# Four tiles of a graph layer summed from gathered rows by GpSimd and VectorE, not by products on TensorE

## The reference

```python
# graph part, x is (6250, 256), a self loop is added to every node
deg = segment_sum(ones, dst);  dis = rsqrt(deg);  norm = dis[src] * dis[dst]
for l in range(2):
    x_res = x
    h = x @ W[l]
    agg = segment_sum(norm[:, None] * h[src], dst) + b[l]
    x = relu(agg + x_res @ resW + resb)
# expert part, on layernorm(x): 6 experts of three 256x256 products, top 2
rh = relu(features @ router_w1 + router_b1)
top_w, top_i = top_k(softmax(rh @ router_w2 + router_b2), 2)
combined = sum(expert_out[top_i] * softmax(top_w))
```

## Time and profile before

| | |
|---|---|
| median of 3 runs | 2027.67 us (2026.81 to 2027.71) |
| profiled execution | 2028.8 us, its span 2027.2 us |
| TensorE busy | 1845.7 us of the span |
| VectorE busy | 1120.7 us |
| ScalarE busy | 771.5 us |
| GpSimd busy | 387.4 us |
| moved by DMAs | 412.55 MB, 124.85 MB of it from GpSimd's queue |

### The profile page before, as it was taken

One profiled execution on the slowest core, in us unless ns is written; L12 is line 12 of the kernel. 1 busy time (PEld: TensorE's weight loads), 2 busy tenths in 40 slices (PEclk: granted clock), 3 DMA queues, 4 the chain that ended last, 5 costly groups with the idle time before them and its releaser, 6 DMA issues. The chain is left out here.

```text
span 2027.2 us, 34554 instructions
## 1 busy us (share of the span) xinstructions
PE 1845.7 (91%) x11170; PEld 1128.0 (56%) x11170; DVE 1120.7 (55%) x2788; ACT 771.5 (38%) x1686; POOL 387.4 (19%) x403
## 2 busy tenths in 40 slices
PE   4448799999999999999959999999999988998886
PEld 3336555555555555555524445444454476886775
DVE  7246766666666666666504444444444566644443
ACT  2226755665566655665501222222222232221221
POOL 1680000000000000000000211111211133335664
PEclk8769899999999999999979999999999999998998
DMA  6255399998999972323364555444555556767783
GB/s 221 58 85 111 106 330 308 285 333 257 293 293 272 282 248 94 153 108 134 154 274 159 184 193 203 173 174 170 184 202 196 186 183 200 253 214 234 256 254 123
DMA packets 121920, 412.55 MB, mean 204 GB/s; under 512 B 14633, under 2 KB 75009, under 8 KB 115577
## 3 DMA queue, kind: packets, MB, share of 16 engines
q1 hardware_dynamic: 82936, 283.65, 40.2%
q0 software_dynamic: 37904, 124.85, 21.9%
q10 hardware_dynamic: 1008, 3.21, 0.4%
HBM read 201.60 MB, written 219.99 MB: 208 GB/s over the span
## 5 line engine op out<-in xcount | busy, mean ns | idle before, releaser
L1383 PE MATMUL bank<-parts,counts 128*128 128x512 f16 x2401 | 643.3, 378 | 0.0
L1383 PE MATMUL bank<-parts,counts_again 128*128 128x512 f16 x2401 | 540.3, 381 | 18.5 <-DMA counts_again<-counts_table 18.5
L1547 ACT ACTIVATE counts<-bank 128x392 f16<-128x392 f32 x800 | 395.1, 497 | 311.2 <-PE bank L1463 304.5
L1383 PEld LDWEIGHTS bank<-parts,counts_again 128*128 128x128 f16 x2401 | 234.1, 99 | 288.4 <-issue 17.0
L594 DVE TENSOR_TENSOR rows_lo<-pair_keys,iota_lo 128x2048 bf16<-128x2048 bf16 x200 | 244.9, 1225 | 239.4 <-PE bank L1463 239.3
L1463 PEld LDWEIGHTS bank<-rows_hi,rows_lo 128*128 128x128 bf16 x3200 | 227.6, 99 | 203.7 <-issue 27.1
L1463 PE MATMUL bank<-rows_hi,rows_lo 128*128 128x98 bf16 x3200 | 277.8, 210 | 11.3 <-DVE rows_hi L594 10.5
L1383 PEld LDWEIGHTS bank<-parts,counts 128*128 128x128 f16 x2401 | 192.5, 96 | 103.6 <-issue 1.1
L454 POOL DMA_INDIRECT first_rows<-route_rows,route_spot_i x49 | 47.9, 977 | 825.7 <-DVE tokens L445 817.7
L594 DVE TENSOR_TENSOR rows_hi<-pair_keys,iota_hi 128x1568 bf16<-128x1568 bf16 x200 | 193.5, 967 | 0.0
L2261 DVE TENSOR_SCALAR h_t<-bank,counts_again 128x256 f32<-128x256 f32 x120 | 57.7, 483 | 161.4 <-PE bank L2097 115.6
(11 more groups left out here) (259 smaller groups left out, 1843.1 us busy)
## 6 DMA issues: line engine op xcount, KB each, us to landing
counts_table<-counts SPq DMA_DIRECT2D x25, 3136.0 KB, 13.7
counts_again<-counts_table SPq DMA_DIRECT2D x24, 3136.0 KB, 11.4
counts_again<-expert_pack SPq DMA_DIRECT2D x60, 898.0 KB
first_rows<-zero_rows POOLq DMA_DIRECT2D x3, 10530.0 KB, 58.4
second_rows<-zero_rows POOLq DMA_DIRECT2D x3, 10449.0 KB, 70.2
res_tile<-res_table SPq DMA_DIRECT2D x98, 128.0 KB, 6.5
first_rows<-zero_rows POOLq DMA_DIRECT2D x1, 10270.0 KB, 61.8
second_rows<-zero_rows POOLq DMA_DIRECT2D x1, 10191.0 KB, 66.7
```

The source lines that it names most:

```text
L1383: mm = nc.tensor.matmul(acc[:, 0:2 * dim], lhs, rhs, start=s == 0, stop=s == tiles)
L1547: nc.scalar.activation(counts[:, b, :, :].rearrange("p s (o n) -> p o s n", o=2)[:, :, :, q * QUAD:(q + 1) * QUAD], bank[4 + q % 4][:, 0:Q ...
```

## The change

Pairs 18 and 20 (`GATHERED`, the tiles 36, 37, 40 and 41) get no one-hot rows, no counts and no products with counts, in either layer. Instead:

- A table `message_table[l]` in DRAM holds the messages in 32 bits (6,272 rows of 256, and 128 rows of zeros). For layer 0 it is written in the preparation: GpSimd adds `rest` and the high half of each tile (49 additions of 128x256), and SyncE stores the result in 7 chunks. For layer 1 the node update stores its scaled row too (one more DMA of 128 KB per tile).
- For each of the four tiles, 56 slots of source nodes (`source_of`) are made from a gathered run of the edge list; unused slots point to a row of zeros. GpSimd's queue then fetches the rows: per layer 28 groups of 8 indirect DMAs (128 rows of 1 KB each), 224 in all, and 4 direct ones for the self loops, into a ring of 3 buffers (`fetch_group`). VectorE sums each group and the running sum in one reduction over the slots of a 128 x 9 x 256 buffer (`sum_group`, 28 per layer).
- In layer 0 VectorE sums two groups per pair in the pairs 2 to 15. In layer 1 GpSimd issues four groups first and then one or two after each pair's scatters.
- The update and the routing of the gathered tiles stay, and are placed among the products of the pairs 19, 21 and 22 by a list written out by hand; the row buffers of the router become three, with a second PSUM bank.
- The packing of the weights moves from GpSimd in the preparation to SyncE at the start of layer 0. The large stores of zeros are gone: the experts' tables have one block of zero rows in front of each region (12 small DMAs), and an expert's last block starts earlier, so that it reads no row that was not written.

The core of the diff:

```diff
+    GATHERED = (18, 20)
+    BACK = 2 * len(GATHERED)
+    RUN = 56
+    LATE = GATHERED[0]
...
+        SLOTS, RING = 8, 3
...
+        def fetch_group(pool, ring, l, n):
+            g = l * GROUPS_ALL + n
+            m, T = tile_of(g)
+            if g >= RING:
+                pool.wait_ge(ring_summed, g - RING + 1)
+            pool.sem_inc(pool_link, 1)
+            if g % GROUPS_OF == 0:
+                pool.dma_start(ring[:, g % RING, 0, :], message_table[l][T * P:(T + 1) * P, :]).then_inc(ring_filled[g % RING], 16)
+            for k in range(SLOTS):
+                at = g % GROUPS_OF * SLOTS + k
+                pool.indirect_dma_start(ring[:, g % RING, k + 1, :], None, message_table[l],
+                                        bass.IndirectOffsetOnAxis(ap=source_of[:, m, at:at + 1], axis=0)).then_inc(ring_filled[g % RING], 16)
+
+        def sum_group(dve, ring, l, n):
+            g = l * GROUPS_ALL + n
+            m, T = tile_of(g)
+            dve.wait_ge(ring_filled[g % RING], fills(g))
+            if g > 0:
+                dve.wait_ge(ring_summed, g)
+            to = gathered_sums[:, m, :] if g % GROUPS_OF == GROUPS_OF - 1 else ring[:, (g + 1) % RING, 0, :]
+            nc.vector.tensor_reduce(to, ring[:, g % RING, :, :].rearrange("p s d -> p d s"), AX, ALU.add).then_inc(ring_summed, 1)
...
+                def message_row(t):
+                    pool.wait_ge(rest_ready, t + 1)
+                    nc.gpsimd.tensor_tensor(feat[:, t, :], rest[:, t % 4, :], parts[:, t, 0:dim], ALU.add).then_inc(message_made, 1)
+                    pool.wait_ge(message_made, t + 1)
...
                 def rest_of(t):
                     dve.wait_ge(high_ready, t + 1)
-                    if t >= 2:
-                        dve.wait_ge(middle_ready, t - 1)
...
+                    if t >= 4:
+                        dve.wait_ge(middle_ready, t - 3)
+                        dve.wait_ge(message_made, t - 3)
...
     def store_next(self, eng, T, o):
         eng.wait_ge(self.res_out, T + 1)
+        eng.wait_ge(self.messages_ready, T + 1)
...
+        eng.dma_start(self.message_table[self.l + 1][bass.ds(T * P, P), :], self.scaled[:, o, :]).then_inc(self.res_stored[o], 16)
...
+            GROUPS_BESIDE = range(2, 2 + GROUPS_ALL // 2)
...
+                            if n in GROUPS_BESIDE and r in (2, 6):
+                                sum_group(dve, ring, 0, 2 * GROUPS_BESIDE.index(n) + (r == 6))
...
                     update.load(sp, 0, 0, 0)
+                    pack_weights(sp)
                     store_counts(0, 0)
...
                 @block.gpsimd
                 def _(pool):
-                    store_zeros(pool)
+                    for n in range(GROUPS_ALL):
+                        fetch_group(pool, ring, 0, n)
                     update.wait_stored(pool)
...
+        LATE_ROUTES = {19: ((17, ROUTE_AT), (18, (92, None, None, None))),
+                       21: ((18, (None, 6, 14, 34)), (19, (44, 52, 60, 92))),
+                       22: ((20, (4, 12, 20, 40)), (21, (50, 58, 66, 94))),
+                       23: ((22, ROUTE_AT),),
+                       24: ((23, ROUTE_AT[0:3] + (None,)),)}
...
+        FIRST_GROUPS = 4
+
+        def groups_behind(p):
+            first = FIRST_GROUPS + (3 * p + 1) // 2
+            return range(min(first, GROUPS_ALL), min(FIRST_GROUPS + (3 * p + 4) // 2, GROUPS_ALL))
+
+        def groups_beside(i):
+            if i in (1, 2):
+                return range(2 * i - 2, 2 * i)
+            return groups_behind(i - 3)
...
+                    for n in range(FIRST_GROUPS):
+                        fetch_group(pool, work.ring, 1, n)
+                    for p in range(LAST_PAIR - 1):
+                        router.scatter(pool, p, buffer_of(p), 2)
+                        for n in groups_behind(p):
+                            fetch_group(pool, work.ring, 1, n)
```

More of the change, by code:

```diff
@@ L1582, in pair @@
[L1582 to L1587 removed]
+                                    update.turned_copy(act, first, 0)
+                                if q == (30 if gathered_tiles else 28):
+                                    update.high_part(act, first, 0, pair_at(n - 1))
+                    for n in range(4):
+                        pair(n, n // 2, n % 2)
```

779 lines of the change are left out of this document (511 added, 268 removed).

## The result

The changed kernel takes 2212.8 us (median of 4 runs, 2200.22 to 2225.03) against 2027.69: 1.0896 times as long, with a 95% interval of [1.0854, 1.0938]. The forecast was 1958 with a range of 1925 to 2130; the time lies above it.

What follows compares the result with a forecast made beforehand. TensorE's list was taken to bound both layers. From 2028.8 us, savings of 55.1 and 43.2, plus 4 for layer 1's start and 24 for late releases, gave 1958.5, predicted as 1958; range 1925 to 2130.

Steps and rivals of the forecast that it cites:

- Late releases, 24 us: Layer 0: ScalarE's copies released late beside 28 groups of eight gathers, 0.86 us each, 24 us in all.
- point (c): Layer 1's scatters, four indirect DMAs in a row, showed no late releases in the trace before the change.
- The same step in layer 1: 0 us: Layer 1: late releases charged nothing, as a released sum has 11 us; 24 more allowed in the range.
- layer 1 hides all 28: Layer 1: VectorE, busy in only 265 of 596 us, absorbs its 28 new reductions at no cost.
- The reduction's length, 2.6 us: VectorE: one reduction of 2,304 elements takes 2.6 us by the longer row, 4.1 by the Trainium skill's hopping rule.
- the 9 to 17 feared: Layer 0: loss if reductions take longer, 9 us at 3.8 us each or 17 at 4.1; 0 was taken.
- TensorE's savings, 98.3 us: Products dropped for two gathered pairs save 55.1 us in layer 0 and 43.2 in layer 1.
- SyncE, 0 us: Start of layer 0: 52 DMAs ahead of the first store of counts, 0.47 us each, cost 0, up to +10.
- The preparation, 0 us: Preparation: GpSimd's 49 new additions and the moved weights cost 0 in all, range -8 to +8.
- The start of layer 1, 4 us: Start of layer 1: 14 gathers, 1.8 MB, arrive beside the data TensorE waits for; +4 us, 0 to +8.
- rival 2: GpSimd bounds layer 1, its indirect DMAs slowed to 1.6 us beside VectorE's two-input operations; 1995 us; 13%.
- rival 1: Late releases bound both layers and make the kernel slower, between 2033 and 2400 us, most below 2150; 26%.

Runs made afterwards that it cites:

- e16: e15 with four kinds of fetch per layer, one per tile (plain, direct, 16-byte rows, 64 rows, pauses); 2095.36 us, 1.0318 times the kernel before.
- e1: The changed kernel without any fetches, the ring filled once with zeros, reductions and waits kept; 1960.35 us against 1963.43 for the kernel before, ratio 0.9981.
- e12: e8 with layer 1's first reduction of a pair moved ahead of shift_logits; 1926.82 us against 1958.88 for the kernel before, ratio 0.9832.
- e7: The changed kernel with the reduction over nine neighbouring elements in place of slots 1 KB apart; 2170.81 us, 39 us less than e6.
- e15: The changed kernel with weights packed by GpSimd after layer 0's last gather and layer 1's first reduction moved; 1899.54 us against 1961.79 for the kernel before.
- e5: The kernel before, unchanged, traced on the same machine as e6; 2022.1 us, with 2030.72 the median of the 7 runs beside it.
- e6: The changed kernel, unchanged, traced on the same machine as e5; 2210.16 us, 1.0877 times the kernel before.
- e8: The changed kernel with the 52 DMAs of the weights issued by GpSimd ahead of layer 0's gathers; 2206.36 us, 1.0864 times the kernel before.

## Why the prediction was wrong, step by step

- **Late releases, 24 us: this step failed.** It charged 0.86 us for each of 28 rows of eight gathers in layer 0, and nothing in layer 1, because a released sum has half a pair, 11 us, of slack. Between the stores of counts at 341.9 and 782.3 us, the twelve pairs of layer 0 beside 24 rows of eight gathers took 440.4 us in place of 377.3: 63 us, or 2.6 us per row, three times the price. The rows held as many gathers as those that the price was taken from (10 to 15 us long here, 9 to 11 there), so a longer row is not the explanation. The price itself was too low: the 68 issues in the expert blocks' window of 113 us were not 8.5 rows of eight but six rows of seven or eight and others of one to four, which by the prediction's own point (c) cost nothing; shared among six rows, 7.3 us are 1.2 us each. What makes the other factor of two was not found.
- **The same step in layer 1: 0 us, the larger error.** A pair took 9.6 us more, 163 us over 17 pairs. GpSimd's rows there are of 12 to 20 indirect DMAs and up to 26 us long, the lateness reached 12 us, more than the slack, and the router's chain has three such replies per pair, not one. In e16 the pairs beside direct DMAs took 23.8 us and those beside plain gathers 33.8 and 33.3, both with the reductions moved, so late releases alone are enough for all of it. The clue stood in the prediction itself: in the preparation the lateness grew with the row of gathers.
- **VectorE: "layer 1 hides all 28" failed too, as B shows.** Counting busy time (265 of 596 us) said nothing of where the reduction stands. It stood ahead of `gates`, `place` and the next pair's `normal_rows`, for which TensorE waits at unit 34. Without any gather, pairs took 26.7 us in place of 23.3, 58 us in all (e1), and moving the reduction by one step gave it back (e12). Part of the 3.4 us is no wait but the granted clock, 0.95 in place of 0.99, after the gaps. On A this loss does not add to the late releases (e7, e16). The reduction's length, 2.6 us, was mis-sized: 4.1 us. Layer 0 held that without loss on B (31.45 us per pair in e1, against the 9 to 17 feared), but on A a reduction of 2.5 us made layer 0 some 25 us shorter (e7).
- **TensorE's savings, 98.3 us: right as a mechanism.** Layer 0 issues 23 stores in place of 25, 31.44 us apart where nothing disturbs. On B, with the weights packed last and the reductions moved (e15), the kernel is 62 us faster: layer 0 took 759.7 us and layer 1 559.9, against 801.7 and 587.8 of the kernel before (traced on A, where neither layer has a late release). Part of what is missing is the longer preparation, 23.9 against 23.3 us per pair of layer 1, and the start of layer 1.
- **SyncE, 0 us: mis-sized.** 0.47 us per issue became 1.03 in e1. That the queue backs up behind its own transfers is likely, but no run shows it. The loss was 21 us on B, 11 beyond the bound; on A the third store came 108.5 us after layer 0's start in place of 81.3, 27 us later, the first row of gathers included.
- **The preparation, 0 us: the bound of 8 held, just.** It grew by 2.7 us in the traces of the result and by 8.2 between e5 and e6 (first one-hot rows at 226.4 and 234.6 us). An addition on GpSimd took 0.74 us.
- **The start of layer 1, 4 us: mis-sized.** From the last store of counts to the first product with loaded counts it took 38.0 us in place of 29.4, and 39.3 on B in e15.
- **GpSimd as bound of layer 1 (rival 2): not seen.** Gathers took 0.95 us there at a spacing of 1.25, and 1.21 in layer 0, beside the one-hot operations.
- **The account by stages.** Layer 0 lost 27 us up to its third store, 63 beside rows of eight and 9 at its end, 99 of the 100.0 in the table; layer 1 lost 163 of its 171.9 in its 17 pairs. With the 2.7 and 6.5 us of the other stages, 2028.8 - 98.3 + 281.1 = 2211.6, the profiled execution's 2211.5. This is an account of one trace by stages, not a forecast. The time lay above the stated range; rival 1, with 26%, had named the cause and the interval in which it fell, though "most of it below 2150" was too low.

## What to carry to other kernels

Divide a loss only among the events that can have caused it, and do not carry the price of a disturbance from one stage to another whose engines wait for each other in another way: rows of eight cost 1.2 us in one stage here and 2.6 in another. Slack covers a lateness only if the lateness cannot outgrow it, so ask what the longest row will do. Two losses measured one at a time need not add: where one hides the other, removing the smaller gives nothing. An operation added to an engine that is half idle costs nothing only if it stands in one of its waits; look up which instruction on the critical chain is queued behind it. A loss that depends on the machine needs the reference timed beside every kernel, and several kinds of one suspected cost inside one kernel (e16) tell in a single run what one kind per run does not, as long as each kind's rows last as long as the others'.

## What the runs showed of the hardware

On A machines, rows of indirect DMAs on GpSimd's queue delayed what TensorE releases to ScalarE and VectorE, by up to 12 us in layer 1's rows with starts 1.25 us apart (the changed kernel), and TensorE itself then stopped too (40.7 us of "issue" before layer 1's products, none before the change). Gathers of 16-byte rows cost TensorE 11 of 118 us and gathers of 64 rows 31 of 135; direct DMAs of the same bytes cost 0 of 94 and gathers with 0.85 us between them 0 of 126 (e16). A row of 24 gathers with starts 1.73 us apart cost nothing (0.2 of 29.5 us), one with 1.33 us did (a wait of 14.3 us in e8). On B machines none of this was seen with the same instructions. What in the machine differs was not found.
